# Column-tiled projections in the layout of a recurrence, and half of each MLP moved behind the last head

## The chip, the cores and the metric

The kernel runs on one core of one Trainium2 chip. The metric is device time in microseconds of that core, the median of the runs. The profile is one further execution of the same program.

## The reference

Sixteen sequences (B = 16) of 128 tokens and 256 channels go through four layers, each with a context `ctx` of the same shape. All arithmetic is float32.

- Layers 0 and 2 are RWKV blocks. A layer norm is followed by a token shift; five mixtures of each token and its predecessor come from a low-rank product (tanh of a 256 x 160 product, then a 32 x 256 product per mixture). From four of them come a decay w = exp(-exp(time_decay + tanh(xw @ decay_w1) @ decay_w2)) and the projections r, k, v (256 x 256 each), from the fifth a gate g. In 32 heads of size 8 a recurrence runs over the tokens: a = k v^T, out = r (u a + s), s = a + w s. The output is normed per head, gated, projected and added to x. A channel mix (three 256 x 256 products, squared relu, sigmoid) follows.
- Layer 1 is cross attention with 16 heads of size 16, added to x through tanh(gate).
- Layer 3 is cross attention with biases, then an MLP: layer norm, 256 -> 1024, gelu, 1024 -> 256, added to x.

```python
w = time_decay + jnp.tanh(xw @ decay_w1) @ decay_w2
w = jnp.exp(-jnp.exp(w)).reshape(B, L, H, S)
r = (xr @ Wr.T).reshape(B, L, H, S)      # k, v in the same way
...
y = jax.nn.gelu(y @ fc_w + fc_b, approximate=True)
y = y @ proj_w + proj_b
return residual + y
```

## The kernel before

The sequences are worked on in four groups of four. For each pair (layer of the kernel 0 or 1, group 0 to 3), eight steps in all, there are three strands of work on every engine: **H**, the head of an RWKV block (norm, mixtures, decay, K, V, R, gate); **R**, its recurrence and what follows (with the channel mix in kernel layer 1); **A**, the cross attention (with the channel mix before it in kernel layer 0 and with the MLP behind it in kernel layer 1). Each strand is a generator in the code of each engine, and one string of letters per engine (`ORDER`, line 100) says which strand's next piece is issued: "HHRA..." means two pieces of the head, one of the recurrence, one of the attention. `in_order` (line 129) reads it. The strings are written by a planner. The queues are in order, so a piece that waits holds up all that stands behind it on its engine, of whatever strand.

Tiles: `PA` (two PSUM banks) belongs to the head, `PB` to the recurrence, `QA` and `QB` (banks 0 to 3 by `bank(i)`) to the attention. `X5` are two buffers of a mixed input, `thT` and `low` low-rank results, `Gt` holds decay and later gate, `K_`, `V_`, `R_`, `W_` [128 x 8 x 128] are the operands of the recurrence: partition = sequence and head (4 x 32), then index inside the head, then token.

**The head** (TensorE line 1088, VectorE 494, ScalarE 840). For each of decay, K, V, R: `maa` (line 1096) multiplies 32 rows of low-rank values into `PA`; VectorE adds and multiplies (`mix_low_rank`, lines 425 and 435) and writes the mixed input, with the columns cut into blocks of 32 tokens of each sequence (`blocks`); TensorE projects (lines 1144 and 1165), the tokens as the stationary operand and the weights as the moving one, so that tokens come out on partitions; VectorE turns blocks of 32 x 32 (`turn`, line 450) so that head and sequence are on partitions, and the next `maa` may overwrite `PA`. For the decay, ScalarE then takes the exponential twice (lines 856 and 860). The matrices' columns are permuted on the host so that the index inside the head comes first (`perm`).

**The recurrence** (VectorE line 555) forms outer products (465), scans (571), multiplies by R (579); TensorE sums over the state with identity matmuls (1198).

**The attention** runs 16 jobs (a sequence and four of the 16 heads each): mask and scores (1279, 1285, 1288), maximum (664), exponentials (972), transposes (1301), copies (981), and after each four jobs the product with V (1312), which is column-tiled: four matmuls with a 32-column stationary operand at `tile_position=(0, 32 * i)`. After all jobs come the output projection (`token_pair`, line 1047, records under 1052 and 1045 for the bias) and the addition to X (708 or 710). The sums of the exponentials are spread and applied after 8 and after 16 jobs (`normalise`, 679).

**The MLP** stands at the end of the attention of kernel layer 1, for all four sequences: norm (389, 397), transposes (1030), `fc` (1364, 512 columns a matmul), gelu (1016), `proj` (1373), addition (725), store (370). In the last attention `fill` issues matmuls without use (1086), which keep TensorE's clock up. In the profile each float32 matmul has two records on TensorE, each with a weight load of its own (PEld); transposes and bf16 matmuls have one.

## Time and profile before

| | us |
|---|---|
| median of 3 runs | 1226.01 |
| lowest, highest | 1220.34, 1228.6 |
| the profiled execution's own time | 1226.18 |
| its span, first to last instruction | 1224.3 |
| TensorE busy (matmuls) | 1108.3 |
| VectorE busy | 839.5 |
| ScalarE busy | 501.6 |
| mean granted clock of TensorE | 0.933 |

Busy times are unions of the records of an engine. A clock of 1 is 2.4 GHz, and the other level is half of it. Idle time is put down to what ended it ("<-DVE A L579": until VectorE had written A on line 579); "issue" is time in which the engine waited for nothing that the profile shows.

### The profile page before, as it was taken

Reading aid. Unit: us, or ns where it says so; the run is one execution under the profiler, and the core shown is the slowest. Engines: PE = TensorE matmul, PEld = TensorE weight load, DVE = VectorE, ACT = ScalarE, POOL = GpSimd, SP = SyncE. Lnnn points to the kernel's source line nnn. Section 1 sums busy time; section 2 is a strip of 40 time slices with the busy share of each in tenths; the row PEclk is TensorE's granted clock in tenths of the full one; section 3 lists DMA queues with packets and bytes.
Section 4 is the critical chain, followed back from the end, with each engine's and each line's share of the span. In section 5 each row is a group of like instructions: output and inputs, shape, how many; then the busy total and the mean of one; then the engine's idle time right before and its main releaser. Section 6 shows DMA issues by size and latency. Waiting matters only on the chain.

```text
span 1224.3 us, 14170 instructions
## 1 busy us (share of the span) xinstructions
PE 1108.3 (91%) x5312; PEld 746.4 (61%) x5312; DVE 839.5 (69%) x1142; ACT 501.6 (41%) x1543; POOL 99.2 (8%) x92
## 2 busy tenths in 40 slices
PE   6858989899889999987999989999999999999888
PEld 4634647556665666664766666665766666666665
DVE  5697689756986689779885589536895378942220
ACT  1003226622573135711574254433544326443741
POOL 1021010001010011001010011000110001100000
PEclk9978889989898889998999889999999999999899
DMA  9100000000000000000000000000000000000000
GB/s 369 51 1 0 1 27 5 1 1 26 6 1 1 18 9 6 1 0 19 13 1 1 26 5 1 1 18 26 5 1 1 18 27 5 1 3 14 14 1 18
DMA packets 13894, 22.64 MB, mean 18 GB/s; under 512 B 3841, under 2 KB 10625, under 8 KB 13186
## 3 DMA queue, kind: packets, MB, share of 16 engines
q1 hardware_dynamic: 13826, 21.74, 5.3%
q8 instruction: 42, 0.69, 0.2%
q14 instruction: 26, 0.21, 0.1%
HBM read 16.48 MB, written 2.10 MB: 15 GB/s over the span
## 4 chain that ended last, share of the span: by engine, by line
PE 63%; DVE 24%; ACT 7%; issue 3%; POOL 1%; DMA 1%; SPq 0%; DVEq 0%; ACTq 0%; POOLq 0%
DVE S_ L571 8%; PE PA L1165 7%; PE PB L1198 5%; PE QA L1373 5%; PE PB L1052 5%; PE QA L1052 4%; PE PA L1102 4%; ACT big L972 4%; DVE A L579 3%; PE QB L1285 3%; PE QB L1039 3%; DVE A L465 3%; DVE nmax L664 2%; PE QA L1301 2%; PE QA L1039 2%
## 5 line engine op out<-in xcount | busy, mean ns | idle before, releaser
L972 ACT ACTIVATE big<-QB,nmax 128x128 f32<-128x128 f32 x512 | 181.4, 376 | 104.9 <-DVE nmax L664 104.6
L1198 PE MATMUL PB<-A,common_w 128*128 128x256 f32 x512 | 136.3, 411 | 22.2 <-DVE A L579 22.1
L571 DVE TENSOR_TENSOR_SCAN S_<-W_,A 128x1024 f32<-128x1024 f32 x64 | 155.4, 2444 | 0.2
L1198 PEld LDWEIGHTS PB<-A,common_w 128*128 128x128 f32 x512 | 100.8, 208 | 44.0 <-DVE A L579 27.2
L664 DVE TENSOR_REDUCE nmax<-QB 128x4 f32<-128x512 f32 x128 | 86.9, 684 | 57.2 <-PE QB L1285 40.5
L972 ACT ACTIVATION_READ_ACCUMULATOR big<-QB,nmax 128x1 f32 x512 | 110.2, 215 | 0.0
L1165 PE MATMUL PA<-rwkv_w,X 128*128 128x256 f32 x384 | 100.3, 419 | 9.1 <-DVE X L435 9.0
L1285 PE MATMUL QB<-big,QX 128*128 128x256 f32 x384 | 100.1, 383 | 0.0
L1165 PEld LDWEIGHTS PA<-rwkv_w,X 128*128 128x128 f32 x384 | 80.3, 213 | 29.6 <-DVE X L435 11.6
L1301 PE MATMUL QA<-common_w,big 128*128 128x128 f32 x512 | 82.4, 285 | 15.1 <-ACT XT L981 8.0
L425 DVE SCALAR_TENSOR_TENSOR PA<-PA,rwkv_w,SX 128x512 f32<-128x512 f32 x80 | 58.7, 755 | 45.4 <-PE PA L1102 43.0
L1301 PEld LDWEIGHTS QA<-common_w,big 128*128 128x128 f32 x512 | 62.3, 145 | 41.0 <-issue 20.5
L1285 PEld LDWEIGHTS QB<-big,QX 128*128 128x128 f32 x384 | 74.5, 194 | 12.7 <-issue 1.3
L465 DVE TENSOR_TENSOR A<-K_,V_ 128x2032 f32<-128x2032 f32 x32 | 72.4, 2262 | 4.1 <-PE PA L1165 3.4
L1102 PE MATMUL PA<-low,rwkv_w 32*128 32x512 f32 x128 | 69.9, 667 | 5.2 <-DVE V_ L450 2.4
L579 DVE TENSOR_TENSOR A<-R_,S_ 128x2048 f32<-128x2048 f32 x32 | 73.0, 2282 | 0.4
L1279 PE MATMUL QB<-mrow,first_row 128*128 128x512 bf16 x128 | 51.2, 400 | 23.0 <-ACT big L972 21.9
L1373 PE MATMUL QA<-mlp_w,big 128*128 128x256 f32 x256 | 59.1, 384 | 1.6 <-ACT big L1016 1.6
L981 ACT ACTIVATE XT<-QA 128x512 f32<-128x512 f32 x64 | 38.9, 607 | 44.3 <-PE QA L1301 44.3
L1373 PEld LDWEIGHTS QA<-mlp_w,big 128*128 128x128 f32 x256 | 47.5, 190 | 12.8 <-ACT big L1016 3.2
L435 DVE TENSOR_TENSOR X<-PA,XN 128x512 f32<-128x512 f32 x80 | 51.4, 684 | 1.1
L1052 PE MATMUL QA<-attn_w,CT 128*128 128x256 f32 x192 | 45.3, 384 | 2.1 <-ACT az L996 2.1
(180 smaller groups left out, 1778.0 us busy)
## 6 DMA issues: line engine op xcount, KB each, us to landing
rwkv_w<-in_rwkv_w SPq DMA_DIRECT2D x2, 2674.0 KB, 13.7
QX<-big SPq DMA_DIRECT2D x96, 32.0 KB, 1.9
attn_w<-in_attn_w SPq DMA_DIRECT2D x2, 1031.5 KB, 15.9
mlp_w<-in_mlp_w SPq DMA_DIRECT2D x1, 2052.0 KB, 23.5
X<-in_x SPq DMA_DIRECT2D x4, 512.0 KB, 13.3
ctx<-in_ctx SPq DMA_DIRECT2D x4, 512.0 KB, 3.4
ctx<-in_ctx_t SPq DMA_DIRECT2D x4, 512.0 KB, 3.5
out<-XT SPq DMA_DIRECT2D x8, 256.0 KB, 2.0
```

The costliest lines, as they stand in the source:

```text
L465: return v.tensor_tensor(A_[c % 2][:, :, :, 1:T], K_[:, :, 0:T - 1].unsqueeze(1).broadcast_to([P, DC, RS, T - 1]), V_[:, DC * c:DC * c + D ...
L571: last = v.tensor_tensor_scan(S_[:, d].rearrange("p k t -> p (k t)"), W_[:].rearrange("p k t -> p (k t)"), A_[c % 2][:, d].rearrange("p k ...
L579: v.tensor_tensor(A_[c % 2][:], R_[:].unsqueeze(1).broadcast_to([P, DC, RS, T]), S_[:], ALU.mult)\
L664: v.tensor_reduce(nmax[:, n % 2], bank(2 + n % 2).rearrange("p (j s) -> p j s", j=JH), AX.X, ALU.max, negate=True).then_inc(sem["a_max"], 1)
L972: last = s.activation(PR[:, n % 2, j], bank(2 + n % 2)[:, j * T:(j + 1) * T], ACT.Exp, bias=nmax[:, n % 2, j:j + 1], accum_out=den[:, b, h ...
L1052: last = t.matmul(dst[:, b * C:(b + 1) * C], lhs(h, b), w[:, h], start=(h == 0 and b == 2 * k), stop=(h == HALF - 1 and bias is None), ski ...
L1102: t.matmul(pa(h), w2, tt, start=True, stop=True, tile_position=(rows, 0)).then_inc(sem["r_maa"], 1)
L1165: last = t.matmul(PA[:, a * C:(a + 1) * C], src[:, h, a * P:(a + 1) * P], wt[:, h], start=(h == 0 and a == 2 * k), stop=(h == HALF - 1), s ...
L1198: last = t.matmul(y, ident, A_[c % 2][:, :, k], start=(c % 2 == 0 and k == 0), stop=False, skip_group_check=True)
L1285: last = t.matmul(o, QX[b % 2][:, i, h], K2[:, :, h, b * T:(b + 1) * T], start=False, stop=True, skip_group_check=True)
L1301: last = t.transpose(bank(0)[:, j * T:(j + 1) * T], PR[:, n % 2, j], ident)
L1373: t.matmul(o, H_[:, m, b * T:(b + 1) * T], proj[:, m], start=(m == 0), stop=False)
```

## The change

1. **K, V, R and decay.** TensorE takes 32 columns of the weights as the stationary operand and the 128 tokens of one sequence as the moving one, at `tile_position=(0, 32 * b)` for the four sequences b, 8 such sets for the 8 indices inside a head. The results stand in `PA` as the recurrence wants them. `turn` and `blocks` go. ScalarE copies K, V, R out of `PA` in halves (6 pieces), and takes the decay's first exponential from `PA`. `r_turned` is now signalled by ScalarE; the waits for free `K_`, `V_`, `R_`, `Gt` move with it.
2. **Output projection in halves.** The projection of sequences 0 and 1 and its addition to X come after job 10 of the attention, in `bank(1)`, which the product with V shares; the product of job 12 waits for that addition (`a_x0`).
3. **The MLP in halves.** Sequences 2 and 3 stay behind their attention (256 columns a matmul, two `fc` tiles per bank). Sequences 0 and 1 become a new unit "mlp" per group; the four of them run in strand H after the last head, in the head's buffers, with stores of their own.
4. `fill` goes from the attention (the first head keeps its own).
5. The four strings of `ORDER` are new throughout. H has 172 letters on TensorE (144 before), 108 on ScalarE (48), 138 on VectorE (190). Of the 28 H pieces of the new units on TensorE, 7 stand before the last letter R and 21 behind it.

```diff
@@ head, TensorE
-                    for a in range(TB):
-                        last = t.matmul(PA[:, a * C:(a + 1) * C],
-                                        thT[0:DEC + 1, a * P:(a + 1) * P],
-                                        r_(L, "dw2")[0:DEC + 1, :], start=True, stop=True)
-                        if a % 2:
+                    for k in range(RS):
+                        for b in range(NB):
+                            last = t.matmul(PA[RH * b:RH * b + RH, k * T:(k + 1) * T], r_(L, "dw2")[0:DEC + 1, RH * k:RH * k + RH],
+                                            thT[0:DEC + 1, b * T:(b + 1) * T], start=True, stop=True, tile_position=(0, RH * b))
+                        if k % 4 == 3:
                             last.then_inc(sem["r_decay"], 1)
...
-                        for k in range(2):
-                            if k:
+                        for k in range(RS):
+                            if k == RS // 2:
                                 yield
                             for h in range(HALF):
                                 if k == 0:
                                     mixed(f + 1)(h)
-                                for a in (2 * k, 2 * k + 1):
-                                    last = t.matmul(PA[:, a * C:(a + 1) * C], src[:, h, a * P:(a + 1) * P], wt[:, h],
-                                                    start=(h == 0 and a == 2 * k), stop=(h == HALF - 1), skip_group_check=True)
-                            last.then_inc(sem["r_proj"], 1)
+                                for b in range(NB):
+                                    last = t.matmul(PA[RH * b:RH * b + RH, k * T:(k + 1) * T], wt[:, h, RH * k:RH * k + RH],
+                                                    src[:, h, b * T:(b + 1) * T], start=(h == 0), stop=(h == HALF - 1), tile_position=(0, RH * b))
+                            if k % 4 == 3:
+                                last.then_inc(sem["r_proj"], 1)
@@ head, ScalarE
+                    for k in range(2):
+                        act.wait_ge(sem["r_decay"], u.at("r_decay", k + 1))
+                        s.activation(E_[:, RS // 2 * k:RS // 2 * (k + 1)], rows_of(k), ACT.Exp).then_inc(sem["r_turned"], 1)
...
+                    for n, dst, free in ((1, K_, "r_out"), (2, V_, "r_y"), (3, R_, "r_rs")):
+                        for k in range(2):
+                            yield
+                            if k == 0 and u.prior:
+                                act.wait_ge(sem[free], u.at(free, 0))
+                            act.wait_ge(sem["r_proj"], u.at("r_proj", 2 * (n - 1) + k + 1))
+                            s.activation(dst[:, RS // 2 * k:RS // 2 * (k + 1)], rows_of(k), ACT.Copy).then_inc(sem["r_turned"], 1)
@@ attention, TensorE
-                        if b and b % 2 == 0:
-                            pe.wait_ge(sem["a_on"], u.at("a_on", b // 2))
+                        if b == 2:
+                            pe.wait_ge(sem["a_x0"], u.at("a_x0", 1))
...
+                    def output(k):
+
+                        pe.wait_ge(sem["a_on"], u.at("a_on", k + 1))
+                        token_pair(bank(1), ah_(L, "Wo"), lambda h, b: CT[:, h, b * T:(b + 1) * T], k, lambda h: None,
+                                   1 if mlp else None, 2 * k).then_inc(sem["a_o"], 1)
@@ attention, VectorE
+                        if n == 10:
+                            yield
+                            x_ready(u, 0 if mlp else 1)
+                            update(0).then_inc(sem["a_x0"], 1)
@@ the new unit, TensorE (fc_two: two matmuls of 256 columns; proj_one: eight and the bias)
+                def first_mlp(u):
+                    yield
+                    pe.wait_ge(sem["m_z"], u.at("m_z", 1))
+                    turn_two(lambda h: PA[:, 512 * h:512 * h + 256], z, 0, sem["m_xT"])
+                    for m in range(FFT):
+                        if m % 2 == 0:
                             yield
                             if m >= 4:
+                                pe.wait_ge(sem["m_gelu"], u.at("m_gelu", m // 2 - 1))
+                        fc_two(PA[:, 256 * (m % 4):256 * (m % 4) + 256], m, m_x,
+                               lambda h: pe.wait_ge(sem["m_xc"], u.at("m_xc", h + 1)), sem["m_fc"])
+                    for b in range(2):
+                        yield
+                        proj_one(PA[:, b * C:(b + 1) * C], lambda m: m_h[m][:, b * T:(b + 1) * T],
+                                 lambda k: pe.wait_ge(sem["m_gelu"], u.at("m_gelu", max(k + 1, 3))), b, sem["m_mlp"])
@@ order
-    programs = {"H": chain(head, MIXERS), "R": chain(recurrence, MIXERS), "A": chain(attn, ATTENTIONS)}
+    programs = {"H": chain((head, MIXERS), (first_mlp, MLPS)), "R": chain((recurrence, MIXERS)), "A": chain((attn, ATTENTIONS))}
```

## Rows read from the trace of the kernel before

**Rows 1.** The page: busy time of TensorE and VectorE, and the chain by engine.

```profile
PE 1108.3 (91%) x5312; PEld 746.4 (61%) x5312; DVE 839.5 (69%) x1142; ACT 501.6 (41%) x1543; POOL 99.2 (8%) x92
PE 63%; DVE 24%; ACT 7%; issue 3%; POOL 1%; DMA 1%; SPq 0%; DVEq 0%; ACTq 0%; POOLq 0%
```

**Rows 2.** The cores: span and mean granted clock.

```profile
core 0: 1224.3 us, clock 0.933
```

**Rows 3.** Stretches: length; PE, PEld, DVE, ACT, POOL busy us (instructions); clock; DMA.

```profile
0.00:40.00 40.00, 30.71 (x136) 21.72 (x137) 19.76 (x41) 6.96 (x10) 4.96 (x14) 0.91 0.83 321
40.00:560.00 520.00, 456.29 (x2084) 304.22 (x2082) 409.14 (x525) 195.46 (x593) 50.16 (x36) 0.90 0.02 6
560.00:1120.00 560.00, 530.30 (x2587) 358.27 (x2588) 387.70 (x531) 251.50 (x772) 41.65 (x38) 0.96 0.04 10
1120.00:1224.30 104.30, 91.00 (x509) 62.18 (x507) 22.87 (x49) 47.71 (x170) 2.40 (x4) 0.93 0.03 10
```

**Rows 4.** What TensorE waited for longest: us in total, times, longest.

```profile
PE PB L1198 <- DVE A L579: 22.1, 8, 7.1
PE QB L1279 <- ACT big L972: 21.9, 31, 2.9
PE PA L1165 <- DVE X L435: 9.0, 4, 3.3
```

**Rows 5.** Groups of TensorE by line and shape: busy us, mean ns.

```profile
L1165 PE MATMUL PA<-rwkv_w,X 128*128 128x256 f32 x384 | 100.3, 419 | 9.1 <-DVE X L435 9.0
L1312 PE MATMUL QA<-XT,VA 128*32 128x128 f32 x512 | 35.9, 285 | 0.7 <-ACT CN L981 0.7
L1144 PE MATMUL PA<-rwkv_w,thT 65*128 65x256 f32 x64 | 15.5, 385 | 1.4 <-ACT thT L851 1.4
L1364 PE MATMUL QB<-XT,mlp_w 128*128 128x512 f32 x64 | 29.4, 592 | 0.0
L1086 PE MATMUL PA<-common_w 128*128 128x128 f32 x62 | 7.5, 277 | 0.0
```

**Rows 6.** A piece of the chain: one whole projection, start us, us.

```profile
404.77 3.45 PE PA L1165 x16
```

**Rows 7.** Timeline of TensorE: a column-tiled burst at the higher clock.

```profile
1054.44 0.38 PE L1198 MATMUL PB<-A,common_w 128*128 128x256 f32 x1
1054.75 0.30 PE L1312 MATMUL QA<-XT,VA 128*32 128x128 f32 x2
1054.88 0.28 PE L1312 MATMUL QA<-XT,VA 128*32 128x128 f32 x2
...
1055.55 0.28 PE L1312 MATMUL QA<-CN,VA 128*32 128x128 f32 x2
1055.76 0.65 PE L1321 MATMUL QA<-common_w,az 128*128 128x128 f32 x4
```

**Rows 8.** Groups of VectorE and ScalarE by line and shape.

```profile
L450 DVE STREAM_TRANSPOSE K_<-PA 128x512 f32<-128x512 f32 x16 | 11.3, 713 | 25.7 <-PE PA L1165 25.5
L981 ACT ACTIVATE XT<-QA 128x512 f32<-128x512 f32 x64 | 38.9, 607 | 44.3 <-PE QA L1301 44.3
L856 ACT ACTIVATE Gt<-Gt 128x1024 f32<-128x1024 f32 x8 | 8.5, 1063 | 21.6 <-DVE Gt L450 21.6
L1016 ACT ACTIVATE big<-QB,mlp_w 128x512 f32<-128x512 f32 x16 | 10.9, 689 | 21.8 <-PE QB L1364 21.8
L1016 ACT ACT_TABLE_LOAD x4 | 5.1, 1283 | 0.1
```

**Rows 9.** Busy time while the last attention runs alone.

```profile
1161.00:1169.00 8.00, 7.32 (x65) 5.48 (x66) 2.80 (x5) 7.58 (x37) 0.00 (x0) 1.00 0.01 2
```

**Rows 10.** Timeline of TensorE: a column-tiled burst at the lower clock.

```profile
1175.45 0.43 PE L1312 MATMUL QA<-XT,VA 128*32 128x128 f32 x2 [0.69 <-ACT CN L981]
1175.66 0.43 PE L1312 MATMUL QA<-XT,VA 128*32 128x128 f32 x2
```

More of the change, by code:

```diff
@@ L70 @@
 PER_GROUP = 6
[L71 removed]
+X_BEFORE = {("mixer", 0): 0, ("attn", 0): 1, ("mixer_ffn", 1): 3, ("attn_mlp", 1): 5, ("mlp", 1): 6}
 class Unit:
@@ L129, in in_order @@
-def in_order(engine, head, recurrence, attn):
-    def chain(unit_program, units):
-        for unit in units:
-            yield from unit_program(unit)
-    programs = {"H": chain(head, MIXERS), "R": chain(recurrence, MIXERS), "A": chain(attn, ATTENTIONS)}
+        "HHHHHHRHHHHHHRRHRRRHRHHHARAAHAHHHAAAAHHAAAAAAAAAAAARAAAAAARAAAAAAHAARARHRAAHRAAAAAAAAHHRAAAHHAHHHHHA"
+        "AAAAAAAAAAARAAAAAHRAAAAAAAARAHARRAAAHARAAAAHHHAAAAAAHHARHHAAAHHAAHAAAAAARAAAAAARAAAAAAARARAHRAAAAAHA"
+        "AAHARRHAAAAHHHAAAAAHHHAHAAAHAAAARAAAAAARAAAAHRAAARRAHAAARHAAAAHHAAAAAARHHAAAAAARAHRHRRAAAHHAAAAAARAA"
@@ L136, in in_order, with chain @@
+def in_order(engine, head, recurrence, attn, first_mlp):
+    def chain(*parts):
+        for unit_program, units in parts:
+            for unit in units:
+                yield from unit_program(unit)
+    programs = {"H": chain((head, MIXERS), (first_mlp, MLPS)), "R": chain((recurrence, MIXERS)), "A": chain((attn, ATTENTIONS))}
     for program in programs.values():
@@ L700, in attn @@
                     yield
[L701 to L711 removed]
+                    update(1).then_inc(lane_sem["x_done"][u.lane], 1)
                     if not mlp:
@@ L1051, in token_pair @@
                         for b in (2 * k, 2 * k + 1):
-                            last = t.matmul(dst[:, b * C:(b + 1) * C], lhs(h, b), w[:, h], start=(h == 0 and b == 2 * k),
+                            last = t.matmul(dst[:, (b - base) * C:(b - base + 1) * C], lhs(h, b), w[:, h], start=(h == 0 and b == 2 * k),
                                             stop=(h == HALF - 1 and bias is None), skip_group_check=True)
@@ L1378, in _ @@
-                in_order("TensorE", head, recurrence, attn)
+                                pe.wait_ge(sem["m_gelu"], u.at("m_gelu", m // 2 - 1))
+                        fc_two(PA[:, 256 * (m % 4):256 * (m % 4) + 256], m, m_x,
+                               lambda h: pe.wait_ge(sem["m_xc"], u.at("m_xc", h + 1)), sem["m_fc"])
+                    for b in range(2):
+                        yield
+                        proj_one(PA[:, b * C:(b + 1) * C], lambda m: m_h[m][:, b * T:(b + 1) * T],
+                                 lambda k: pe.wait_ge(sem["m_gelu"], u.at("m_gelu", max(k + 1, 3))), b, sem["m_mlp"])
@@ L1381 @@
+                in_order("TensorE", head, recurrence, attn, first_mlp)
 def kernel(**inputs):
```

289 lines of the change are left out of this document (149 added, 140 removed).

## The prediction

> **What bounds the kernel now.** I began with the page's busy times and its chain by engine [rows 1]. The reader is to see that TensorE is busy for 1108.3 of 1224.3 us and holds 63% of the chain of waits; VectorE is second in both (839.5 us, 24%), and ScalarE is far behind (501.6 us, 7%). TensorE is the bound, but its busy share hides a second loss: the mean granted clock is 0.933 [rows 2], so for 0.067 x 1224.3 = 82 us of the span TensorE lacked half of its pulses, spread over stretches at 1.2 GHz in place of 2.4. An ideal order would have some 1108 - 82 = 1026 us of work left to do at the full clock; the 116 us of idle time and the 82 us of clock are what a better order can win from.
>
> Next the stretches [rows 3]. From 0 to 40 us the loads run, and nothing of the change touches that. From 40 to 560 us (the first layer) TensorE is idle for 520 - 456.3 = 63.7 us at clock 0.90, with VectorE at 79%: both engines take turns. From 560 to 1120 us it is idle for 29.7 us only, at 0.96. From 1120 us the last attention and the last MLP stand alone: 13.3 us idle, clock 0.93, and 62 matmuls that only keep the clock up, 7.5 us of them [rows 5]. The waits of TensorE say who is late [rows 4]: the product of R and S for the recurrence (22.1 us, VectorE), the exponentials (21.9 us, ScalarE), and the mixed input of a projection (9.0 us, VectorE).
>
> **The change, part by part.** The sum is made against the profiled execution (span 1224.3 us, time 1226.2 us, so 1.9 us lie around it); the median shown is 1226.0, so no correction is needed.
>
> *Projections.* A projection of K, V or R has 8 matmuls of 256 columns, 16 records of TensorE, 3.45 us where nothing disturbs it [rows 6]. It becomes 8 x 2 x 4 = 64 matmuls with a 32-column weight and 128 moving columns, 128 records, four tiles side by side. The attention's product with V has this very form: 4 records start together, the next 4 start 0.13 us later, and 32 records go from 1054.75 to 1055.55 us, 0.80 / 7 = 0.11 us for each four [rows 7]. So a projection takes 32 x 0.11 = 3.52 us, +0.07 each, 24 of them +1.7 us. The decay has 8 records of 256 columns (64 / 8 heads) at 15.5 / 8 = 1.94 us [rows 5]; after, 32 matmuls, 16 fours, 1.76 us: -1.4 us in all. The way into and out of the column tiles costs a little: 1054.75 - 1054.44 = 0.31 us to the first tile where 256 columns take 3.45 / 16 = 0.22, and 0.21 us out of it against 0.11, so 0.2 us a burst [rows 6, 7]. A head has 4 bursts, 7 where the yields cut them, 6.4 to 11.2 us over 8 heads; I take 8. Bounds of the whole part: 0 (if the switch already made for the neighbouring row-tiled matmul is shared) and, if the tiles did not overlap at all, 3584 records (24 x 128 + 8 x 64) at (0.65 - 0.28) / 3 = 0.12 us, as the four full-width ones behind the burst have it [rows 7], instead of 0.0275: +332 us. I take +8 in all, from the row of the same form.
>
> The Trainium skill, TensorE: Matmul & The Clock Gate, section Part 3, gives three column tiles a measured speedup of 2.38, 79% of ideal. By that, each four would take 0.11 x 3 / 2.38 = 0.139 us and the 896 fours (24 x 32 + 8 x 16) some 26 us more. Our rows, 0.11 us for four against 0.12 for one full-width record of as many columns, disagree for this short burst, and I stay with them.
>
> *VectorE is relieved.* 64 transposes of 0.71 us go [rows 8], 45 us or 5.4% of its work, 5.7 us a head. ScalarE takes 48 copies (0.607 us each, 29.1 us) and 16 exponentials straight from PSUM (about the same, 9.7 us) for 8 of 1.063 us (8.5): +30 us on an engine that was 41% busy. In the chain of one step a 0.71 us transpose becomes a 0.61 us copy, so a lone head gains almost nothing (under 0.5 us); the gain is that VectorE can run scans and products while the copies are made. Bounds: 0, and 45 us of VectorE plus the clock that the idle time costs. Half of the 45 lies where VectorE is late (stretch 40 to 560 and the recurrences after): I take -16 us of TensorE's idle time and -6 us of clock (0.10 x 520 = 52 us are lost there, and a ninth comes back), together -22, and +3 for copies that stand behind exponentials in ScalarE's queue.
>
> *The end.* The MLP is cut in two. The half of sequences 0 and 1 of each group becomes a unit of its own after the last head; the output projection of that half is moved in among the attention's jobs, after job 10. The columns are the same (fc in 256 instead of 512 columns, twice as many), so TensorE's work is not changed; 29 us of MLP per group becomes two parts of 14.5, of which three or four now lie beside the last attention. That stretch is bound by ScalarE when alone (7.58 of 8.00 us) while TensorE's records, ends included, fill 7.32 [rows 9]. What can be won after 1120 us: 13.3 us idle, of which 3.4 (last addition and store) stay and 3 stay as latency, -7; the fillers, 7.5 us, nearly all, -7; of the clock's 0.07 x 104.3 = 7.3 us a good half, -4. Sum -18. Bounds: -25, and +10 if ScalarE takes the stretch (third rival).
>
> *Added waits.* The values product of job 12 now waits until VectorE has added the first half of the output to X (one 0.69 us addition, two jobs earlier in the order). What is queued behind it on TensorE is everything, other units too. Two jobs are nearly 4 us, which covers normalisation, projection and addition. SP's Q spreads are not passed by anything: the stores of the first halves stand behind the spreads of the last attention, and each has its own room. Uncovered it would cost 1 to 2 us in each of 8 attentions. Against that, half of the end of each attention (normalise, project, add) leaves the chain. I take -6 in all, bounds +12 and -15.
>
> Sum: +8 - 22 + 3 - 18 - 6 = -35 us, and 1226 - 35 = 1191; I say 1190 us.
>
> **The rivals.**
> *Tail only.* VectorE's relief is worth nothing, because the order is in balance with TensorE. For it: TensorE is the bound and a lone step is no shorter. Against it: the 22.1 us wait on VectorE. Time 1226 + 8 - 18 - 6 = 1210 us.
> *ScalarE takes it back.* Its queue is in order, and a job of the attention fills it (7.58 of 8.00 us [rows 9]). If each pair of copies waits half a job, 0.95 us, for 4 steps of 6 heads that meet an attention, that is 23 us; the gelus among exponentials load tables, 1.283 us each [rows 8], perhaps 12 more, half of them on the path, 8 us. 1190 + 31 = 1221 us, no change.
> *The clock falls in the bursts (slower).* Place: all 32 bursts of the heads. The same burst at the lower clock takes 0.21 us per four (1175.66 - 1175.45) instead of 0.11 [rows 7, 10], so 98 us of bursts (24 x 3.52 + 8 x 1.76) would become 188, +90, of which a tenth is paid today: 1190 + 80 = 1270 us. It decides from some 36 / 80, 45% of the bursts at the lower clock. For it: the one burst of the last attention's end ran at the lower clock. Against: TensorE had waited 0.69 us just before it [rows 10], and the burst near 1055 us kept the higher one to its end.
> *The bursts outrun the supply of instructions.* No burst now is longer than 32 records; the new ones have 64 to 128. The gain is gone when a record costs 36 / 3584 = 0.010 us more, 0.0375 in place of 0.0275. Between 0.0275 and the 0.12 of full-width records [rows 7] I take the middle, +0.046 x 3584 = +165: 1355 us. The Trainium skill, TensorE: Matmul & The Clock Gate, section Part 1, says that with hardware decoding off the sequencer needs about 62 ns per matmul; by that page the estimate is +124 us. The short burst agrees with the other case, but its records could have been queued beforehand, so no row excludes it.
> *Not what it says:* the tiles serialise, the +332 above; I give it no more than 1 in 100, within the last rival.
>
> **How the numbers follow.** Chances: forecast 0.58 (own range 1165 to 1213), tail only 0.13, ScalarE 0.13, clock 0.10, supply 0.06. About 1% (12 us) is what a measurement of this kernel can tell from no change. Faster: 0.57 + 0.10 = 0.67; same: 0.01 + 0.03 + 0.11 = 0.15; slower: 0.02 + 0.10 + 0.06 = 0.18. The range reaches down to 1150, where all of the VectorE relief (45) and the tail's bound (25) would come in part, and up to 1240, past the ScalarE case; outside it lie 0.05 below and 0.15 above, the last two rivals.
>
> **What would show it.** Right: the new projection groups at 32 fours of 0.11 us each; VectorE near 795 us busy, ScalarE near 535 or more; idle time of TensorE after 40 us from 107 us to about 80; mean granted clock above 0.94; the 22.1 us wait on line 579 smaller; after the last recurrence TensorE nearly without gaps. Wrong: a four at 0.13 us or more in mid-burst, TensorE's busy time above 1120 us, a clock under 0.92, or waits of VectorE and TensorE on the new ScalarE copies of more than 20 us in sum.

## The result, and the profile after

The changed kernel takes 1217.62 us, the median of 20 runs (1216.18 to 1222.56), beside 1227.66 for the kernel before in the same session. The ratio is 0.9939, with a 95% interval of 0.9924 to 0.9954; the two medians by themselves lie 10.0 us apart. By the interval the change is worth 6 to 9 us where the forecast had 35. The ratios in this document leave out two runs that took far longer than all others, one of the kernel before (6064.32 us) and one of e9 (1648.96 us, at a clock of 0.63).

The page of the changed kernel, busy times and the chain by engine (answering to [rows 1]):

```profile
PE 1096.4 (90%) x8514; PEld 765.5 (63%) x8514; DVE 795.6 (65%) x1078; ACT 545.7 (45%) x1648; POOL 115.1 (9%) x100
PE 62%; DVE 21%; ACT 9%; POOL 3%; issue 3%; DMA 1%; SPq 0%; DVEq 0%; ACTq 0%; POOLq 0%
```

The view of its cores, span and mean granted clock (to [rows 2]):

```profile
core 0: 1217.2 us, clock 0.954
```

VectorE fell by 43.9 us, to 795.6, and the clock rose from 0.933 to 0.954, as foreseen. ScalarE rose by 44.1 us where the sum had 30: the gelus take 4.6 us more (32 pieces of 512 columns became 64 of 256), and ScalarE loads its function tables 31 times instead of 22, at 1283 ns each, 11.5 us more. The largest part of the loads is new among the exponentials, before and after:

```profile
L972 ACT ACT_TABLE_LOAD x4 | 5.1, 1283 | 0.1
L990 ACT ACT_TABLE_LOAD x12 | 15.4, 1283 | 0.2
```

TensorE is idle for 1217.2 - 1096.4 = 120.8 us, against 116.0 before. With 44 us less to do for VectorE, TensorE's idle time did not fall at all.

The stretches, in the same columns as [rows 3], say where:

```profile
0.00:40.00 40.00, 33.87 (x324) 24.67 (x325) 20.00 (x41) 8.18 (x13) 4.97 (x14) 0.96 0.83 321
40.00:560.00 520.00, 447.96 (x3825) 302.94 (x3824) 378.73 (x483) 209.14 (x620) 57.48 (x36) 0.92 0.02 6
560.00:1120.00 560.00, 524.73 (x3823) 366.62 (x3822) 376.53 (x514) 271.56 (x826) 49.97 (x44) 0.98 0.04 10
1120.00:1217.20 97.20, 89.82 (x548) 71.29 (x546) 20.32 (x43) 56.78 (x190) 2.67 (x6) 0.99 0.05 16
```

The end came as worked out: idle time 13.3 to 7.4 us, the clock from 0.93 to 0.99 (7.3 to 1.0 us lost), the fillers gone (7.5). That is 19.7 us of losses gone from that stretch, where the sum had 18. The part ahead of it went the wrong way in idle time: from 40 to 560 us TensorE is idle for 72.0 us instead of 63.7, and from 560 to 1120 for 35.3 instead of 29.7, 13.9 us more together. The clock went the right way in both, by 0.02 each, which is 10.4 + 11.2 = 21.6 us less lost where the sum had 6.

The waits of TensorE (to [rows 4]):

```profile
PE PB L1263 <- DVE A L563: 31.5, 14, 9.4
PE QB L1337 <- ACT big L990: 21.4, 28, 2.9
PE PA L1229 <- DVE X L450: 7.1, 9, 3.2
```

The first is the wait that the relief of VectorE was to shorten, 22.1 us in [rows 4]. It has grown to 31.5 us. The reader is to see that an engine with 44 us less to do is now later than before where it matters. Where VectorE's freed time went stands in its own waits, before and after:

```profile
DVE PA L425 <- PE PA L1102: 43.0, 21, 7.6
DVE PA L441 <- PE PA L1166: 97.9, 26, 17.6
```

It is the wait for TensorE's low-rank product in the head. Before, VectorE also waited in front of its transposes, 56.5 us on top of the 43.0 (K_ 25.5, Gt 12.2, R_ 9.7, V_ 9.1), 99.5 us together. So in the heads VectorE waits for TensorE about as long as it did, only at another piece.

The bursts of the projections and of the decay in the groups of TensorE (to [rows 5]):

```profile
L1229 PE MATMUL PA<-X,rwkv_w 128*32 128x128 f32 x3072 | 98.1, 285 | 7.5 <-DVE X L450 7.1
L1209 PE MATMUL PA<-thT,rwkv_w 65*32 65x128 f32 x512 | 15.6, 274 | 1.4 <-ACT thT L858 1.4
```

One such burst in the timeline of TensorE (start, us; to [rows 6, 7]):

```profile
531.19 3.70 PE L1229 MATMUL PA<-X,rwkv_w 128*32 128x128 f32 x128
534.82 1.12 PE L1166 MATMUL PA<-low,rwkv_w 32*128 32x512 f32 x2
```

And ScalarE's new work, a group of copies and the exponentials of the decay (to [rows 8]):

```profile
L879 ACT ACTIVATE K_<-PA 128x512 f32<-128x512 f32 x16 | 9.4, 604 | 24.3 <-PE PA L1229 24.2
L866 ACT ACTIVATE Gt<-PA 128x512 f32<-128x512 f32 x16 | 9.4, 597 | 12.3 <-PE PA L1209 12.3
```

From the burst's start to the next instruction pass 534.82 - 531.19 = 3.63 us for 32 fours: 0.113 us each, the change of mode included. The pace of the tiles is as forecast (0.11), and so is the price of a copy (0.60 us).

The end shows in the last maximum of the attention and the last additions, by VectorE's timeline of before, then of after:

```profile
1170.71 0.69 DVE L664 TENSOR_REDUCE nmax<-QB 128x4 f32<-128x512 f32 x1 [1.99 <-PE QB L1285]
...
1221.17 0.69 DVE L725 TENSOR_TENSOR XT<-QA,X 128x512 f32<-128x512 f32 x1 [7.03 <-PE QA L1045]
```

```profile
1175.29 0.69 DVE L648 TENSOR_REDUCE nmax<-QB 128x4 f32<-128x512 f32 x1 [0.40 <-PE QB L1343]
...
1213.29 0.69 DVE L707 TENSOR_TENSOR XT<-QA,X 128x512 f32<-128x512 f32 x1 [19.87 <-PE QA L1081]
```

From the last maximum to the last addition of the second half it is 38.0 us, before 50.5, so the end itself became 12.5 us shorter. (The 19.7 us above are more, because the stretch from 1120 us now also holds pieces of the first halves: losses that went were partly filled with work.) The last maximum comes 4.6 us later than before. The end gave most of its share and the part ahead of it took some back.

### The profile page after: what moved, and what is told of

It reads as the page before. It is cut to its first block, busy times and chain, and to the rows that moved or that the text cites. A ratio compares the mean times of both kernels' runs of the same rounds, so it can differ in the third digit from the quotient of the medians.

```text
span 1217.2 us, 20606 instructions
## 1 busy us (share of the span) xinstructions
PE 1096.4 (90%) x8514; PEld 765.5 (63%) x8514; DVE 795.6 (65%) x1078; ACT 545.7 (45%) x1648; POOL 115.1 (9%) x100
## 4 chain that ended last, share of the span: by engine, by line
PE 62%; DVE 21%; ACT 9%; POOL 3%; issue 3%; DMA 1%; SPq 0%; DVEq 0%; ACTq 0%; POOLq 0%
DVE S_ L555 7%; PE PA L1229 7%; PE QA L1116 5%; PE PA L1166 5%; PE PB L1116 5%; PE PB L1263 4%; PE QB L1343 4%; ACT big L990 4%; DVE A L563 3%; PE QA L1359 3%; PE PA L1106 2%; PE QB L1075 2%; PE QA L1106 2%; PE QB L1346 2%; PE QA L1370 2%
## 5 line engine op out<-in xcount | busy, mean ns | idle before, releaser
L1263 PE MATMUL PB<-A,common_w 128*128 128x256 f32 x512 | 136.6, 410 | 31.5 <-DVE A L563 31.5
L555 DVE TENSOR_TENSOR_SCAN S_<-W_,A 128x1024 f32<-128x1024 f32 x64 | 151.2, 2387 | 1.8 <-ACT A L844 1.4
L441 DVE SCALAR_TENSOR_TENSOR PA<-PA,rwkv_w,SX 128x512 f32<-128x512 f32 x80 | 59.1, 754 | 100.3 <-PE PA L1166 97.9
L1229 PE MATMUL PA<-X,rwkv_w 128*32 128x128 f32 x3072 | 98.1, 285 | 7.5 <-DVE X L450 7.1
L1229 PEld LDWEIGHTS PA<-X,rwkv_w 128*32 128x32 f32 x3072 | 86.5, 115 | 19.7 <-DVE X L450 12.8
L1343 PEld LDWEIGHTS QB<-big,QX 128*128 128x128 f32 x384 | 75.3, 196 | 12.8 <-issue 2.6
L1337 PE MATMUL QB<-mrow,first_row 128*128 128x512 bf16 x128 | 50.5, 394 | 21.5 <-ACT big L990 21.4
L1166 PE MATMUL PA<-low,rwkv_w 32*128 32x512 f32 x128 | 63.5, 614 | 1.9 <-ACT low L854 1.9
L1116 PE MATMUL PB<-rwkv_w,S_ 128*128 128x256 f32 x192 | 48.9, 403 | 0.8 <-DVE S_ L590 0.8
L999 ACT ACTIVATE CN<-QA 128x512 f32<-128x512 f32 x64 | 39.0, 609 | 21.2 <-PE QA L1359 21.1
```

The source lines that it names most:

```text
L555: last = v.tensor_tensor_scan(S_[:, d].rearrange("p k t -> p (k t)"), W_[:].rearrange("p k t -> p (k t)"), A_[c % 2][:, d].rearrange("p k ...
L999: s.activation(PT[n % QUAD], bank(0).rearrange("p (j t) -> p j t", j=JH), ACT.Copy)\
L1116: last = t.matmul(dst[:, (b - base) * C:(b - base + 1) * C], lhs(h, b), w[:, h], start=(h == 0 and b == 2 * k), stop=(h == HALF - 1 and bi ...
L1166: t.matmul(pa(h), w2, tt, start=True, stop=True, tile_position=(rows, 0)).then_inc(sem["r_maa"], 1)
L1229: last = t.matmul(PA[RH * b:RH * b + RH, k * T:(k + 1) * T], wt[:, h, RH * k:RH * k + RH], src[:, h, b * T:(b + 1) * T], start=(h == 0), s ...
L1263: last = t.matmul(y, ident, A_[c % 2][:, :, k], start=(c % 2 == 0 and k == 0), stop=False, skip_group_check=True)
```

## The experiments

Two theories stood at first. A: the relief of VectorE is on no path. B: it is worth what I predicted, and something else in the change (the copies, the tiles) eats it. Ratios are to the kernel before in the same session; smaller is faster.

**e1, the relief alone.** The kernel before; zeros are laid into K, V, R and both gate buffers at the start.

```diff
-                        v.transpose(to[:, two], of[:, two]).then_inc(sem["r_turned"], 1)
+                        one = slice(TB // 2 * k, TB // 2 * k + 1)
+                        v.transpose(to[:, one, 0:1], of[:, one, 0:1]).then_inc(sem["r_turned"], 1)
```

> The kernel before, with each of VectorE's 64 transposes behind the decay, K, V and R cut to one 32x32 block (so E, K, V and R hold zeros nearly everywhere; orders, waits and TensorE's work as before). It gives VectorE the relief of the change (about 45 us of busy time) with no load on ScalarE, no column tiles and no new order. Theory A (the relief is on no path: the order in which the pieces stand and the recurrence's own chain set the pace): at most 8 us faster than before, 1217 to 1228 us. Theory B (the relief is worth what I predicted, and something else in the change eats it): about 22 us faster, 1200 to 1208 us. Under both VectorE's busy time falls by 40 to 50 us.

Measured: 1217.14 us, ratio 0.9933 [0.9907, 0.9960], 7.6 us (5 to 11 by the interval). VectorE's busy time fell by 32.5 us only, since 64 short transposes are left, and with them their waits. GpSimd lays the zeros ahead of the first inverse deviation, here in e1's timeline of GpSimd and then in that of before:

```profile
8.77 0.95 POOL L760 MEMSET Gt<- 128x1024 f32 x1
10.09 1.02 POOL L771 TENSOR_TENSOR rstd<-veps,half_pow 128x4 f32<-128x4 f32 x1
```

```profile
6.59 1.01 POOL L760 TENSOR_TENSOR rstd<-veps,half_pow 128x4 f32<-128x4 f32 x1
```

So the first deviation comes 3.5 us late. This delay doesn't last. VectorE of the kernel before waits for a DMA soon afterwards anyway, and TensorE's first low-rank product starts no later in e1. VectorE of before, then TensorE of before and of e1:

```profile
11.72 0.55 DVE L631 CAST big<-big 1x768 bf16<-1x768 f32 x1 [2.63 <-DMA big<-in_bias_w]
```

```profile
24.88 1.98 PE L1102 MATMUL PA<-low,rwkv_w 32*128 32x512 f32 x4
```

```profile
24.24 1.98 PE L1113 MATMUL PA<-low,rwkv_w 32*128 32x512 f32 x4
```

The zeros therefore take nothing from the result, and 32.5 us of relief gave 7.6 us (the 8 to 11 us in the expectation of e5 below added the 3.5, which this trace doesn't bear out). In proportion, 45 us would give 7.6 x 45 / 32.5 = 10.5 us, an estimate, and 16 at the interval's far end. My term of 22 is refuted, and "at most 8" is met within the noise.

**e2, the changed kernel without the copies.** Each copy is cut to one element of each partition. K, V and R hold zeros, laid at the start as in e1. The first inverse deviation comes 8.08 - 6.41 = 1.7 us later, but the first gate product starts at 55.01 us in e2 and at 55.65 in the changed kernel, so this delay doesn't last either.

```diff
-                            s.activation(dst[:, RS // 2 * k:RS // 2 * (k + 1)], rows_of(k), ACT.Copy).then_inc(sem["r_turned"], 1)
+                            s.activation(dst[:, RS // 2 * k:RS // 2 * k + 1, 0:1], rows_of(k)[:, 0:1, 0:1], ACT.Copy).then_inc(sem["r_turned"], 1)
```

> The kernel after, with each of ScalarE's 48 copies of K, V and R cut to one element (K, V and R hold zeros nearly everywhere). It takes back about 29 us of ScalarE's added work and leaves the rest. Theory A (relief of VectorE worth little; ScalarE's copies delay the second projections' successors a little): 1208 to 1217 us. Theory B (ScalarE's copies eat the relief of VectorE): 1195 to 1203 us, and TensorE's waits on ScalarE fall by more than 15 us.

Measured: 1217.99 us, ratio 0.9944 [0.9926, 0.9963], against 0.9939 for the change itself. ScalarE's busy time fell by 20.3 us and nothing was gained, so the busy time of the 48 copies costs nothing that can be measured; by the two intervals it is some 2 us at most. The cut copies keep their places and their waits in ScalarE's queue, so e2 says nothing of copies that come late because they stand behind exponentials, which is how my rival "ScalarE takes it back" had it. That is read from the waits of the changed kernel on copies, first TensorE's, then VectorE's:

```profile
PE PA L1166 <- ACT R_ L879: 0.5, 1, 0.5
```

```profile
DVE A L465 <- ACT V_ L879: 0.3, 1, 0.3
```

No other matmul and no other instruction of VectorE waits for a copy. That is 0.8 us, and the weight loads ahead of the matmuls wait 8.3 us more, mostly beside running matmuls, where the prediction's sign of being wrong was more than 20 us. Theory B in the form "ScalarE takes it back" is out by both.

**e3, the changed kernel without column tiles.** The four-tile loops are replaced by the full-array loops of before.

```diff
-                        for k in range(RS):
...
-                                    last = t.matmul(PA[RH * b:RH * b + RH, k * T:(k + 1) * T], wt[:, h, RH * k:RH * k + RH],
...
+                        for k in range(2):
...
+                                    last = t.matmul(PA[:, a * C:(a + 1) * C], src[:, h, a * P:(a + 1) * P], wt[:, h],
```

> The kernel after, with the decay and the K, V and R projections in four full-array matmuls of 256 columns per pass, as before, instead of bursts of four column tiles (the channels of K, V, R and the decay land in the wrong places; the number of columns passed and the copies stay). Theory A (tiles cost only their changes of mode, about 0.2 us per burst or 9 us in all): 1206 to 1212 us. Rival C (tiles cost the relief, 20 us or more, through slower passes or the clock): 1195 to 1200 us. If they cost nothing: 1214 to 1220 us.

Measured: 1207.63 us, ratio 0.9861 [0.9837, 0.9885]. The tiles cost about 10 us, where the sum had 8. In the groups of e3 the same projections show a part of it:

```profile
L1229 PE MATMUL PA<-rwkv_w,X 128*128 128x256 f32 x384 | 92.1, 391 | 7.1 <-DVE X L450 7.0
```

98.1 us of busy time in the changed kernel, 92.1 here, 6.0 of the 10 us, and the idle time ahead of them is nearly the same, 7.5 and 7.1 us. The rest of the 10 us isn't assigned.

**e4, the first MLP halves last.** The last 12, 4, 12 and 28 letters H of VectorE's, GpSimd's, ScalarE's and TensorE's orders are moved to their ends.

> The kernel after, with every piece of the four first-half MLP units moved behind all other pieces in the written orders of the four engines; the computation is the same. Each unit holds about 16.2 us of TensorE's busy time. Theory A (the end delivered what was predicted, because these pieces fill the gaps of the last attentions): 20 to 40 us slower than after, 1238 to 1258 us. Rival (the pieces only move work around and fill nothing): at most 8 us slower.

Measured: 1280.83 us, ratio 1.0466 [1.0432, 1.0500], 63 us slower than the changed kernel. That is more than my theory's 20 to 40. The chain of e4 (start, us) shows the matmuls of its last two units, one unit behind the other:

```profile
1243.43 8.86 PE PA L1096 x32
...
1264.46 8.78 PE PA L1096 x32
1273.25 3.45 PE PA L1106 x16
1276.91 3.65 PE PA L1106 x16
```

A unit takes 21 us alone, four of them 84 us, and the move costs 63. So in the changed kernel the four units, with 65 us of TensorE's work, lengthen the span by only some 21 us: most of them lies in gaps of the other work. By the pages and cores, TensorE's idle time is 153.9 us in e4 against 120.8, and the clock's loss 0.070 x 1284.0 = 89.9 against 56.0. This compares two places for the units. It doesn't show that cutting the MLP in two is worth anything against the whole MLP of before.

**e5 and e6, each part alone.** e5 is the kernel before with the layout hunks of the change; e6 is the changed kernel with these hunks taken back (its turn pieces begin with the yield, the wait behind it). In both, pieces are put in where the other kernel's trace has their work in time.

> The kernel before with the layout part of the change alone: decay, K, V and R in four column tiles, ScalarE's copies and exponentials out of PSUM, no transposes. The written orders are those of before, with VectorE's 64 transpose pieces taken out and ScalarE's 64 pieces put in at the times at which the transposes began. From the experiments before: relief of VectorE 8 to 11 us (e1_no_turns gave 7.6 for 32 us of busy time), copies nothing (e2_no_copies), tiles +10 (e3_no_tiles). Theory A: these cancel, 1220 to 1230 us. Theory B (the relief needs the tiles' layout to pay, as in my sum of -11): 1209 to 1216 us. Rival D (the copies stand at bad places in ScalarE's queue): 1235 us or more.

> The kernel after with the layout part undone: full-array projections and VectorE's transposes as before, ScalarE's copies gone, the split MLP and the rest kept. The written orders are those of after, with 64 pieces put in on VectorE at the times at which ScalarE's exponentials and copies began, and ScalarE's 48 copies taken out. Theory A (layout is worth nothing net, the split MLP and its orders are the whole gain): 1212 to 1222 us, as after. Theory B (the layout part carries the gain): 1225 us or more.

Measured: e5 1226.74 us, ratio 1.0014 [0.9997, 1.0030]; e6 1243.81 us, ratio 1.0152 [1.0126, 1.0178]. The layout alone is worth nothing, as theory A said, and the parts fit: 7.6 us from the relief (e1) against 10 for the tiles (e3) leave nothing for late copies to take. Rival D's 1235 us did not come. But the split MLP alone is 19 us *slower* than before. That lies in theory B's range (1225 us or more), yet not for its reason, since e5 shows that the layout carries no gain either. Two parts worth +2 and +19 give -7 together. Such a table tells of orders and not of code: the orders of the changed kernel are made for pieces that e6 doesn't have. In e6 TensorE waits for transposes in front of its low-rank product (line 1191):

```profile
PE PA L1191 <- DVE R_ L470: 6.8, 4, 2.9
...
PE PA L1191 <- DVE K_ L470: 5.7, 3, 2.2
...
PE PA L1191 <- DVE Gt L470: 4.1, 3, 1.5
...
PE PA L1191 <- DVE V_ L470: 2.0, 2, 1.5
```

That is 18.6 us, where the kernel before has 3.9 us of this wait (V_ 2.4, Gt 1.5) with the same transposes in its own order. The wait for the recurrence's product, which grew from 22.1 to 31.5 us, also goes with the orders and the split, and not with the layout. It reads in e5, which has the layout and before's orders, and in e6, which has the opposite:

```profile
PE PB L1182 <- DVE A L547: 19.5, 8, 7.1
```

```profile
PE PB L1287 <- DVE A L599: 29.8, 14, 7.8
```

So a third theory: the written orders decide, and the diff replaced all four of them.

**e7 and e8, new orders for both kernels.** No instruction is changed in either. The only edit is the table ORDER; the four strings were searched with a model of the queues.

> The kernel before, not an instruction changed, with the four written orders searched anew by a model of the engines' queues fed with the durations of the traces. Theory A (what decides is the order in which the pieces stand; the orders in place leave idle time that better ones don't): 15 to 60 us faster, 1165 to 1210 us. Rival (the orders in place are as good as this code allows): 1220 us or more.

> The kernel after, not an instruction changed, with its four written orders searched anew in the same way for the same time. Beside the new order of the kernel before it gives the worth of the change's code with orders of equal care. Theory A (after's own orders use little of the relief and of the freedom to place the first MLP halves): the gap between the two grows from 7 to 15 us or more, so 1150 to 1195 us. Rival (the change's code is worth 7 us whatever the order): 5 to 9 us under the other's time.

Measured: e7 1196.38 us, ratio 0.9773 [0.9746, 0.9799]; e8 1146.20 us, ratio 0.9344 [0.9319, 0.9370]. New strings alone take 28 us from the kernel before and 71 us from the changed one, the second more than the 1150 to 1195 us expected.

**e9, e10, e11, the parts under new orders.**

> The kernel of e5_layout_alone (before with the layout part alone), its four written orders searched anew as for e7 and e8. e7 (before) took 1196.4 us and e8 (after) 1146.2: with orders of equal care the change is worth 50 us. Theory A (nearly all of it is the split MLP's freedom of place): 1185 to 1198 us. Theory E (the two parts share it, since VectorE relieved leaves fewer late heads): 1165 to 1180 us.

> The kernel of e6_tail_alone (after with the layout undone), its orders searched anew as for e7 and e8. Theory A: 1140 to 1158 us, as e8 or little more. Theory E: 1165 to 1180 us. Rival F (the split pays nothing without the layout, as e6 at 1244 us hints): 1190 us or more.

> The kernel and orders of e8, with the decay and the K, V and R projections in full-array matmuls as in e3_no_tiles (channels land in the wrong places). e3 gave 10 us less than after. With TensorE idle only 76.7 us of 1144.9 in e8, the tiles' work lies more on the path: 8 to 14 us under e8, 1132 to 1138 us. If the price hung on after's orders alone: within 4 us of e8.

Measured: e9 1173.42 us, ratio 0.9580 [0.9547, 0.9612]; e10 1155.98 us, 0.9454 [0.9435, 0.9473]; e11 1136.83 us, 0.9295 [0.9274, 0.9315]. The tiles cost 9.4 us here and 10 in e3, under quite different orders: that price belongs to the code. e9 came in theory E's range and e10 in theory A's, so neither theory held for both. The rest looked like a clean result (layout -23 or -10, split -40 or -27). It was not one. The model had 32 waits of before's transpose pieces one piece too late (a wait ahead of a yield), so that e7 may have had a handicap.

**e12 to e15, all four combinations again**, with that mended, a longer search and another seed.

> The kernel before with a second, independent new order: a longer search with another seed, and with 32 waits of VectorE's transpose pieces placed in the model where the engine meets them (the first search had them one piece late, which put e7 at a disadvantage). Theory A (the order scatters little between searches): 1180 to 1198 us. Rival G (e7's lag came from that flaw of the model): 1150 to 1175 us.

> The kernel of e5 and e9 (layout part alone) with a second new order from the same longer search. If e9's 1173.4 us tells of the code and not of its order: 1163 to 1180 us, and 10 us or more under e12. Rival G: no faster than e12.

> The kernel of e6 and e10 (split MLP, layout undone) with a second new order from the same search. If e10's 1156.0 us tells of the code: 1145 to 1160 us, and 20 us or more under e12.

> The kernel after with a second new order from the same search. If e8's 1146.2 us tells of the code: 1133 to 1150 us, the lowest of the four. The change's worth with orders of equal care is then e12 minus this one: 30 us or more by theory A; under 20 us by rival G.

**e16, e17, before and after once more**, with only the seed changed.

> The kernel before with a third new order: the search of e12 (1151.3 us) with another seed and nothing else different. It measures how far orders of one search scatter for one code. If they scatter little: 1144 to 1158 us, and the 24 us between e12 and e15 are the code's. If by 10 us or more either way, that difference is mostly chance.

> The kernel after with a third new order: the search of e15 (1127.6 us) with another seed. If orders scatter little: 1121 to 1135 us, so that before and after stay 20 to 28 us apart in both pairs. If the order decides: 1140 us or more.

All medians, in us:

| code | orders of the two kernels (adapted in e5 and e6) | first search | second, seed 1 | second, seed 2 |
|---|---|---|---|---|
| before | 1226.01 | 1196.4 (e7) | 1151.3 (e12) | 1164.1 (e16) |
| layout part alone | 1226.7 (e5) | 1173.4 (e9) | 1147.0 (e13) | |
| split MLP alone | 1243.8 (e6) | 1156.0 (e10) | 1149.9 (e14) | |
| after | 1217.6 | 1146.2 (e8) | 1127.6 (e15) | 1142.1 (e17) |

Ratios of the last six: e12 0.9377 [0.9345, 0.9408], e13 0.9346 [0.9310, 0.9383], e14 0.9366 [0.9347, 0.9386], e15 0.9188 [0.9171, 0.9205], e16 0.9503 [0.9467, 0.9540], e17 0.9323 [0.9293, 0.9353].

e12 came in rival G's range, 45 us under e7. But the mended waits, the longer search and the new seed came together, and the changed kernel, which never had the flaw, gained 19 us from the last two alone (e8 to e15); how much of the 45 the flaw made is not shown. The other expectations of e12 to e15 mostly missed: e13 is 4 us under e12 where 10 or more were expected, e14 1 us where 20 were, and e12 minus e15 is 23.7 us, between theory A's 30 and rival G's 20.

Within one code two seeds of one search lie 12.8 us (before) and 14.5 us (after) apart. Between the codes the pairs lie 23.7 us (e12, e15) and 22.0 us (e16, e17) apart, and e8, e15 and e17 are all under every order of the kernel before. The recorded signs disagree. e16 had said that a scatter of 10 us or more makes that difference mostly chance, and e17 that 1140 us or more means the order decides; both came. That the pairs stay 20 to 28 us apart came too, but a pair shares only a seed number: e12 against e17 would give 9 us, e16 against e15 36.5. So the change's code is probably faster under new orders, by something like 23 us, and neither the size nor, with two orders on each side, the sign is shown beyond doubt. The parts by themselves (e13: -4, e14: -1) are inside the scatter and stay open.

**e18, the relief again, under e12's orders.**

> The kernel and orders of e12_before_order_2 (1151.3 us), with VectorE's 64 transposes cut to one 32x32 block each as in e1_no_turns. In before's own orders that relief of 32 us of busy time gave 7.6 us. e12 leaves TensorE idle for 76.9 us instead of 116.0. If a quarter of VectorE's relief reaches the end whatever the order: 1140 to 1146 us. If only an order made for it can use it: within 4 us of e12, 1147 to 1155 us.

Measured: 1157.18 us, ratio 0.9438 [0.9412, 0.9464], 6 us slower than e12 and just outside both ranges. Here the zeros at the start do cost something: the first product of the recurrence starts at 70.66 us instead of 68.47, 2.2 us late. TensorE's longest waits in e12 and in e18:

```profile
PE QA L1030 <- DVE az L397: 14.0, 5, 4.0
PE PB L1198 <- DVE A L579: 9.8, 2, 6.4
PE QB L1039 <- DVE XT L408: 8.5, 3, 3.7
```

```profile
PE QA L1041 <- DVE az L397: 13.4, 5, 4.5
PE PB L1209 <- DVE A L580: 9.8, 2, 6.4
PE QB L1050 <- DVE XT L408: 8.5, 3, 3.7
```

The reader is to see that they are the same to the tenth, but for 0.6 us in one: 33 us of VectorE's work went out of the middle of its queue, and none of TensorE's long waits on it became clearly shorter. TensorE's idle time is 1155.8 - 1079.5 = 76.3 us against 76.9. In that order the relief is worth nothing. e1 and e18 differ in the orders alone, and the same relief gave 7.6 us in one and none in the other.

**Where the time of the orders lies.** The busy times on the pages of e12, e16, e15 and e17, in this order:

```profile
PE 1070.6 (93%) x5312; PEld 731.0 (64%) x5312; DVE 837.1 (73%) x1142; ACT 506.9 (44%) x1547; POOL 104.7 (9%) x92
```

```profile
PE 1075.8 (93%) x5312; PEld 735.4 (63%) x5312; DVE 843.3 (73%) x1142; ACT 506.7 (44%) x1548; POOL 115.7 (10%) x92
```

```profile
PE 1064.2 (95%) x8514; PEld 754.0 (67%) x8514; DVE 798.6 (71%) x1078; ACT 543.9 (48%) x1646; POOL 113.9 (10%) x100
```

```profile
PE 1069.2 (94%) x8514; PEld 755.8 (66%) x8514; DVE 801.5 (70%) x1078; ACT 545.7 (48%) x1648; POOL 115.3 (10%) x100
```

The spans and clocks below are from the views of the cores. Each span is split into idle time (span minus busy), what the clock took ((1 - clock) x span) and what is left. The split is rough, since the second term also counts the lower clock of idle time:

| kernel | span | clock | idle | lost to the clock | left |
|---|---|---|---|---|---|
| before | 1224.3 | 0.933 | 116.0 | 82.0 | 1026.3 |
| after | 1217.2 | 0.954 | 120.8 | 56.0 | 1040.4 |
| e12 | 1147.5 | 0.958 | 76.9 | 48.2 | 1022.4 |
| e16 | 1162.3 | 0.956 | 86.5 | 51.1 | 1024.7 |
| e15 | 1124.0 | 0.968 | 59.8 | 36.0 | 1028.2 |
| e17 | 1140.5 | 0.962 | 71.3 | 43.3 | 1025.9 |

What is left moves by 18 us at most: it rises by 1 to 6 us from e12 and e16 to e15 and e17, and it is highest in the changed kernel, 12 us over e15 with the same instructions (short stalls that count as busy; its 512 matmuls of the recurrence's product have a mean of 410 ns against 394 in e15). The idle time and the clock make the difference: new orders took 73 us from the two together (before to e12) and 81 us (after to e15). e15 against the changed kernel, the same instructions, in TensorE's wait on the recurrence's product:

```profile
PE PB L1263 <- DVE A L563: 7.4, 2, 6.5
```

and in its group of TensorE that waits for the exponentials:

```profile
L1337 PE MATMUL QB<-mrow,first_row 128*128 128x512 bf16 x128 | 49.2, 384 | 0.4 <-ACT big L990 0.4
```

They were 31.5 and 21.4 us. And the last head's gate is ready earlier; VectorE's timeline of after, then of e15:

```profile
1004.46 1.20 DVE L537 SCALAR_TENSOR_TENSOR Gt<-Gt,PA 128x1024 f32<-128x1024 f32 x1
```

```profile
919.26 1.22 DVE L537 SCALAR_TENSOR_TENSOR Gt<-Gt,PA 128x1024 f32<-128x1024 f32 x1 [0.32 <-ACT Gt L883]
```

e15, the changed kernel with the second new order, beats both: 1127.55 us, 0.9188 of the kernel before.

## Why the prediction was wrong

- **The sum as a whole.** Forecast 1190, measured 1217.6. That is outside the forecast's own range (1165 to 1213) and inside the wide one (1150 to 1240) only by luck: its upper end was there for late copies of ScalarE, which did not come.
- **"VectorE is relieved": the step that failed.** It read: "Half of the 45 lies where VectorE is late (stretch 40 to 560 and the recurrences after): I take -16 us of TensorE's idle time and -6 us of clock". With nothing else changed the chip gave 7.6 us for 32.5 of the 45 (e1; 10.5 by proportion, an estimate), and nothing under another order (e18). The half was taken from a busy share (79% in [rows 3]) and a wait of 22.1 us [rows 4]. Neither says that the removed pieces stand in front of the late one. In e18 they did not stand in front of any that TensorE waited long for. In the changed kernel VectorE spends the freed time waiting for TensorE's low-rank product (97.9 us).
- **"Tail only", the rival nearest in mechanism.** It had the relief at nothing and gave 1210 us, with a chance of 0.13. The relief is nearer to its 0 than to my 22.
- **The step that was missing: the orders.** The diff replaced all four strings of ORDER, and the sum treated them as if they were before's. Their price was bounded by nothing in the text. With searched orders the changed kernel gains 71 to 90 us on its own orders, the kernel before 28 to 75. What counts for the forecast is the difference between the two codes: seed by seed (e15 against e12, e17 against e16) the changed kernel's own orders leave 14 to 15 us more unused than before's do. That is about as large as the rest of the shortfall, but also as large as the scatter between two seeds, so it is likely and not shown. That the wait for the recurrence's product is longer with the new orders and the split (29.8 us in e6) than with the old ones (19.5 in e5) speaks for it.
- **Where it is missing in the split of the span.** TensorE's idle time after 40 us was to fall from 107 to about 80 us and rose to 114.7. What is left beside idle time and clock was to rise by 1 us (tiles +8, fillers -7) and rose by 14.1; runs of the same instructions differ by 12 us there (after, e15), and no run says which stalls these are. The clock gave back 26.0 us, where the sum had some 10. Two misses of 35 and 13 us are partly hidden by one of 16 the other way.
- **Copies, +3.** Right in size: 0 to 2 us (e2). The rival "ScalarE takes it back", whose 1221 us are the nearest number of all, has the wrong mechanism: the waits of matmuls and of VectorE on the copies are 0.8 us. The added table loads that it named came (nine, 11.5 us), and TensorE's wait for the exponentials stayed as it was, 21.9 and 21.4 us.
- **Tiles, +8.** Right in size: 10 us under one order (e3), 9.4 under another (e11); fours at 0.113 us. The rival of the clock is out: its lower level would give the records 0.43 us each [rows 10], they have a mean of 285 ns over all 3072, against 273 in the median, so fewer than one in ten ran there, where it needed 45%. The rival of the instruction supply is out too: the burst above runs 128 records in 3.63 us, 0.028 us each, or 0.057 us for each of the 64 matmuls in the code. The Trainium skill, TensorE: Matmul & The Clock Gate, Part 1, has about 62 ns per matmul with hardware decoding off; nothing here is bound by that. By Part 3 of the same page of the Trainium skill, a speedup of 2.38 for three tiles, the prediction had estimated 0.139 us for a four; the 26 us that it worked out from it are not there.
- **The end, -18.** Right in the losses (19.7 us after 1120 us), and 12.5 us as the length of the end itself. That it can be read alone was not right: in after's orders and without the layout the split kernel came out 19 us slower than before (e6), and under new orders e14 is 1 us from e12. What the split is worth by itself stays open.
- **Early half and added wait, -6.** Not tried by itself; open. Of the added wait the trace shows nothing: in TensorE's waits of the changed kernel no row names the first addition to X (lines 676 and 677).
- **"What would show it".** VectorE near 795 (795.6), clock above 0.94 (0.954) and the fours came. Idle time near 80 us after 40 us (it is 114.7) and a shorter wait on the product (31.5 us) did not, and these two were the ones on which the gain hung.

## What to carry to other kernels

In a kernel whose engines run written orders that take turns, a change of code and a change of order are two changes. Price the order as a term with bounds of its own, and compare codes only with orders of equal care and more than the two seeds each that were tried here, since two seeds of one search lie 13 to 15 us apart, more than any part of this change is worth. Work taken from an engine that isn't the bound counts only if it stands in front of a piece that somebody waits for: look for that piece in the waits, and don't take a share of the busy time. When undoing the parts of a change gives sums that contradict each other, as +2 and +19 against -7, suspect what the parts share.

## What the runs showed of the hardware

Four column tiles of 32 weights and 128 fp32 columns keep their pace through a whole burst of 128 records, 0.113 us for four. A projection in this form takes 3.63 us from its start to the next instruction. The same columns in 16 records of full width take 3.45 us in the chain [rows 6], and 3.55 us where, as behind the burst, the low-rank product follows (TensorE's timeline of before, 527.40 to 530.95 us). In this kernel the form costs 9 to 10 us for 32 bursts (e3, e11), 0.3 us each. The 0.08 to 0.18 us by which this burst is longer is a part of that; where the rest arises no run separates.

Under new orders less idle time of TensorE came with less lost to the clock: from before to e12, the same instructions, 39.1 us and 33.8 us; from after to e15, 61.0 us and 20.0. In part this is one loss counted twice, since the clock's term covers idle time as well. From before to after the clock's loss fell by 26.0 us while the idle time rose by 4.8, so the sum of the idle time alone doesn't set it; where the gaps lie may do it, and no run here separates that.
